# Routing of the second token group spread over chunks 9 to 15, slot positions kept as 16-bit integers

## The chip, the cores and the metric

One core of one Trainium2 chip runs the whole program. The metric is device time in microseconds of one execution. The kernel before takes 329.79 us (median of three runs, 329.2 to 330.83).

## The reference

For x of 32 x 256 tokens of 128 features (8192 tokens):

```python
xn = layernorm(x)
# s: a gated linear recurrence along each sequence of 256 tokens
hidden, gate = split(xn @ W_hg)                # 256 each
h = scan(h' = (1 - sigmoid(gate)) * h + sigmoid(gate) * (relu(hidden) + 0.5))
s = h @ W_out
# g: a shared expert plus the two best of 16 experts for each token
shared = silu(xn @ Sg) * (xn @ Su) @ Sd
p, i = top_k(softmax(xn @ Wr), 2)
routed = sum over the two of p * (silu(xn @ Wg[i]) * (xn @ Wu[i]) @ Wd[i])
out = x + s * silu(routed + shared)
```

(The recurrence is written in log space in the reference; this is what it amounts to.)

## The kernel before

**First stage: 16 chunks of 512 tokens.** PE transposes the normalised tokens, computes the router's logits (`logits`, L897) and six products of 128 x 512 for each chunk (`up`, L911: four for the recurrence, two for the shared expert), and then, one chunk later, the two down products (`rec_down`, L929, and `shared_down`, L941). ACT computes the tanh, relu and copies (`rec_in`, `shared_silu`, `copy_down`). DVE does two scans for each chunk (`rec_scan`, L551: one combining instruction at L555, one scan at L561) and the product of the shared expert (`shared_gated`, L564). The products of `up` go round four PSUM banks, so the fourth product of a chunk, `up(i, 3)`, waits for `shared_gated(i - 1)` (L917 to L925).

**Routing, in the same stage, on DVE.** The tokens are two groups: chunks 0 to 9 (40 tiles of 128 tokens) and chunks 10 to 15 (24 tiles). For each token the two best experts are found in batches of tiles (`route_top`, `route_second`, both through `first_of`, which ends with a `tensor_reduce`, L575 to L608): six and four instructions for a batch. `route_keys` turns the two experts into one of 20 lines (each line is four experts whose weights lie side by side, and any two experts share a line). `count_keys` marks the line of each token and counts along the tiles; `prefix` on PE (L950) sums over partitions; `key_bases` and `positions` turn counts into the row (slot) that each token gets in a table in DRAM. `positions` works on [128, lines, tiles] and ends with a maximum over the lines, read with a step of 24 words (L790). `shift_logits`, ACT's `exponentials` and `probabilities` give the two weights. `tile_keys` says which line each tile of 128 slots uses. For group 1 the two halves' positions are in chunks 7 and 8, for group 2 in chunk 13. What DVE does in which chunk is an order written out by hand (L832 to L874); the routing steps stand in front of the chunk's two scans. DVE, like every engine here, executes its instructions in order.

**Dispatch and slots.** POOL writes each tile's token rows to their slots, one indirect DMA for each tile (`dispatch`, L344), at most four in flight, the 40 of group 1 as soon as its positions are there (`s_pos`), then `block_weights(1)`, then the 24 of group 2, which also need `s_pos` 3. After that POOL stores results (`store_out`, L350), two indirect DMAs for each pair of slot tiles.

**Second stage: 42 pairs of slot tiles.** SP loads pair n from the table into one of RX = 10 buffers (`load_slots`, L255): pair 0 needs all dispatches of group 1, pair 10 all dispatches of group 2, and every pair n of 10 or more needs the stores of pair n - 10 to have landed:

```python
if n == PAIRS0:
    for k in range(WINDOW):
        sp.wait_ge(s_disp[k], 16 * (NT // WINDOW))
if n >= RX:
    sp.wait_ge(s_out[n % RX], 32 * (n // RX))
```

ACT normalises the rows (L457, pair n + 2 in iteration n), PE transposes them (L974) and multiplies with the line's weights (L998), ACT and DVE form the hidden values, PE transposes and multiplies down (L1010, L1023), DVE and ACT make the output rows (L816 to L825), POOL stores them.

Of the kernel before, what the change touches and what calls it, by code (L numbers as in the profile page):

```python
# [5 lines left out]
F32 = mybir.dt.float32  # L6
BF16 = mybir.dt.bfloat16
U32 = mybir.dt.uint32
I32 = mybir.dt.int32
ALU = mybir.AluOpType  # L10
ACT = mybir.ActivationFunctionType
AX = mybir.AxisListType

P = 128
# [50 lines left out]
LINES = 20  # L65
# [9 lines left out]
def recurrent_moe_block(nc, x, W_front, W_tail, W_lines, out, S, E, F):  # L75
# [14 lines left out]
        return min(2, USED - 2 * n)  # L90

    assert SLOTS % 4 == 0 and FULL_TILES * P <= len(TILES[0]) * P - LINES * (P - 1)
    BATCHES = [(0, 12), (12, 20), (20, 28), (28, 36), (36, 40), (40, 52), (52, 64)]
    HALVES = [[(0, 20), (20, 40)], [(0, 24)]]

    x_tiles = x.rearrange("(c t p) d -> c p t d", p=P, t=TT)
# [3 lines left out]
    with ExitStack() as ctx:  # L100
        def sb(name, shape, dt=F32):
            return ctx.enter_context(nc.sbuf_tensor(name, shape, dt))
# [9 lines left out]
        rev = sb("rev", [P, E])  # L112
        iota4 = sb("iota4", [P, BLOCK], U32)
        iota_k = sb("iota_k", [P, LINES], U32)
        tile_row = sb("tile_row", [P, 1])
# [47 lines left out]
        TB = max(b - a for a, b in BATCHES)  # L163
# [4 lines left out]
        r01 = sb("r01", [P, 2, NT])  # L168
        i01 = sb("i01", [P, 2, NT], U32)
        k_a, k_b, k_c, k_d, k_e = (sb(f"k_{n}", [P, TG], U32) for n in "abcde")  # L170
        key = sb("key", [P, NT], U32)
# [4 lines left out]
        oh = sb("oh", [P, LINES, TG + 1], BF16)  # L176
# [8 lines left out]
        base = sb("base", [P, LINES])  # L185
        delta = sb("delta", [P, LINES])
        fresh = sb("fresh", [P, LINES])
        moved = sb("moved", [P, LINES, 24])
        ptmp = sb("ptmp", [P, LINES, 24])
        eq = moved.rearrange("p l t -> p (l t)")[:, 0:TB * E].rearrange("p (t e) -> p t e", e=E)  # L190
        lg2 = ptmp.rearrange("p l t -> p (l t)")[:, 0:TB * E].rearrange("p (t e) -> p t e", e=E)
        pos = sb("pos", [P, NT], U32)
        le = sb("le", [P, 3, LINES])
        tk = sb("tk", [P, 3])
# [20 lines left out]
        s_step = sem("routing_step")  # L215
# [313 lines left out]
        def _(dve):  # L529
# [61 lines left out]
            def route_top(q):  # L591

                nonlocal steps
                a, b = BATCHES[q]
                n = b - a
                revs = rev[:, :].rearrange("p (t e) -> p t e", t=1).to_broadcast([P, n, E])
                dve.wait_ge(s_lgc, b // TT)
                first_of(q, lg[:, a:b], m0, 0)
                nc.vector.tensor_tensor(eq[:, 0:n], revs, per_expert(r01[:, 0, a:b], n), ALU.is_equal).then_inc(s_step, 1)
                dve.wait_ge(s_step, steps + 1)  # L600
                nc.vector.scalar_tensor_tensor(out=lg2[:, 0:n], in0=eq[:, 0:n], scalar=-BIG, in1=lg[:, a:b],
                                               op0=ALU.mult, op1=ALU.add).then_inc(s_step, 1)
                steps += 2
                dve.wait_ge(s_step, steps)

            def route_second(q):
                a, b = BATCHES[q]
                first_of(q, lg2[:, 0:b - a], m1, 1)  # L608
# [42 lines left out]
            def shift_logits(g):  # L651

                t = TILES[g]
                a, b, n = t.start, t.stop, len(t)
                nc.vector.tensor_tensor(p01[:, 1, a:b], m1[:, a:b], m0[:, a:b], ALU.subtract)
                nc.vector.tensor_tensor(lg[:, a:b], lg[:, a:b], per_expert(m0[:, a:b], n), ALU.subtract).then_inc(s_shf, 1)
# [109 lines left out]
            def positions(g, k):  # L766

                nonlocal steps
                a, b = HALVES[g][k]
                n, t0 = b - a, TILES[g].start  # L770
                dve.wait_ge(s_pref, (len(HALVES[0]) if g else 0) + k + 1)

                def per_tile(v):
                    return v[:, :].rearrange("p (l t) -> p l t", t=1).to_broadcast([P, LINES, n])

                prefix = p_lg[:, 0:LINES * n].rearrange("p (l t) -> p l t", l=LINES)
                rank, extra = ptmp[:, :, 0:n], moved[:, :, 0:n]
                nc.vector.tensor_tensor(extra, prefix, per_tile(room), ALU.subtract).then_inc(s_step, 1)
                nc.vector.tensor_tensor(rank, prefix, per_tile(base), ALU.add).then_inc(s_pread, 1)
                dve.wait_ge(s_step, steps + 1)  # L780
                nc.vector.scalar_tensor_tensor(out=extra, in0=extra, scalar=0.0, in1=per_tile(delta), op0=ALU.is_ge,
                                               op1=ALU.mult).then_inc(s_step, 1)
                dve.wait_ge(s_step, steps + 2)
                dve.wait_ge(s_pread, (len(HALVES[0]) if g else 0) + k + 1)
                nc.vector.tensor_tensor(rank, rank, extra, ALU.add).then_inc(s_step, 1)
                dve.wait_ge(s_step, steps + 3)
                nc.vector.tensor_tensor(rank, rank, oh[:, :, 1 + a:1 + b], ALU.mult).then_inc(s_step, 1)
                steps += 4
                dve.wait_ge(s_step, steps)
                nc.vector.tensor_reduce(pos[:, t0 + a:t0 + b], rank.rearrange("p l t -> p t l"), AX.X, ALU.max)\  # L790
                  .then_inc(s_pos, 1)

            def block_gated(n):
# [38 lines left out]
            for i in range(NCH):  # L832
                if 1 <= i <= 5:
                    route_top(i - 1)
                    route_second(i - 1)
                if i == 5:
                    shift_logits(0)
                if i == 6:
                    count_keys(0)
                if i == 7:  # L840
                    key_bases(0)
                    positions(0, 0)
                if i == 8:
                    positions(0, 1)
                if i == 9:
                    tile_keys(0)
                    route_top(5)
                    route_second(5)
                if i == 10:
                    route_top(6)  # L850
                    route_second(6)
                if i == 11:
                    shift_logits(1)
                    route_keys(1)
                if i == 12:
                    count_keys(1)
                if i == 13:
                    key_bases(1)
                    positions(1, 0)
                if i == 14:  # L860
                    tile_keys(1)
                for c in STATS.get(i, []):
                    ln_stats(c)
                rec_scan(i, 0)
                if i == 5:
                    route_keys(0)
                rec_scan(i, 1)
                if read(i):
                    copy_logits(read(i))
                if i == 6:  # L870
                    probabilities(0)
                shared_gated(i)
                if i == 12:
                    probabilities(1)  # L874
            for n in range(PAIRS):
                block_gated(n)
                if n >= 2:
# [234 lines left out]
```

## Time and profile before

| what | value |
|---|---|
| median of the runs | 329.79 us |
| the profiled execution's own time | 327.45 us |
| its span | 325.7 us |
| mean granted TensorE clock | 0.974 |
| busy PE, DVE, ACT, POOL | 90%, 77%, 74%, 62% of the span |
| POOL's 64 dispatches (L348) | 71.4 us busy, 1116 ns each |
| share of the chain that ended last | PE 78%, ACT 5%, issue 5%, POOL 4%, DVE 3% |

```
PE   0699999999989999996968999999999999999920
DVE  7399999999999799999451778787878787878830
ACT  1789999999975777985664777777787878787520
POOL 3997446530137776878667777665656566656670
PEclk9999999999998999998999999999999999999985
```

Each digit is one of 40 equal slices of the span (8.14 us each), the busy share in tenths, 9 for 90% and more; PEclk is TensorE's granted clock in tenths. The first stage ends at about 167 us, in slice 21. "Idle before" and names in brackets say what ended an engine's idle time. Instructions follow each other in pipelines, so the step from one start to the next is what counts, not always the printed duration.

### The profile page before, as it was taken

To read this page: it belongs to the slowest core of one execution; us is meant where nothing else is said; L and a number is where in the kernel's file an instruction comes from. 1 tells how busy PE (TensorE), PEld (TensorE's weight loads), DVE (VectorE), ACT (ScalarE), POOL (GpSimd) and SP (SyncE) were. 2 spreads that over 40 slices of the span, in tenths; PEclk is the share of its full clock that TensorE was granted. 3 is DMA by queue.
4 is the path that set the end of the run, shared out by engine and by line. 5 is a ranking of instruction groups with operands and counts; after the bars stand their busy time and mean duration, and the time that the engine had idled before them with its cause. 6 is when DMAs were issued, how large, how long until landed. Compare 5 with 4: busy or idle time off the path is not lost.

```text
span 325.7 us, 5997 instructions
## 1 busy us (share of the span) xinstructions
PE 291.7 (90%) x1523; PEld 198.5 (61%) x1523; DVE 252.0 (77%) x634; ACT 241.4 (74%) x517; POOL 201.2 (62%) x242
## 2 busy tenths in 40 slices
PE   0699999999989999996968999999999999999920
PEld 0357767766656666663645676777777777777620
DVE  7399999999999799999451778787878787878830
ACT  1789999999975777985664777777787878787520
POOL 3997446530137776878667777665656566656670
PEclk9999999999998999998999999999999999999985
DMA  8999999690006885333795435755656454541000
GB/s 233 303 372 393 440 445 399 228 432 3 0 28 204 279 256 215 124 127 147 247 405 195 168 107 194 208 176 149 180 149 181 150 181 129 168 127 51 19 0 0
DMA packets 28256, 63.62 MB, mean 195 GB/s; under 512 B 3717, under 2 KB 22672, under 8 KB 27456
## 3 DMA queue, kind: packets, MB, share of 16 engines
q1 hardware_dynamic: 21184, 45.58, 41.3%
q0 software_dynamic: 6752, 17.06, 14.2%
q10 hardware_dynamic: 288, 0.60, 0.6%
q8 instruction: 15, 0.25, 0.3%
q14 instruction: 17, 0.14, 0.1%
HBM read 29.32 MB, written 35.14 MB: 198 GB/s over the span
## 4 chain that ended last, share of the span: by engine, by line
PE 78%; ACT 5%; issue 5%; POOL 4%; DVE 3%; DMA 1%; POOLq 0%; ACTq 0%; DVEq 0%
PE p_u L998 21%; PE p_u L926 20%; PE p_s L1023 10%; PE p_s L937 8%; PE p_sh L1010 5%; PE p_lg L907 4%; PE p_sh L946 4%; PE p_xt L974 3%; POOL out L354 2%; PE p_xt L894 2%; DMA arena<-in_x 1%; POOL arena L310 1%; ACT arena L457 1%; ACT rec L427 1%; ACT rec L420 1%
## 5 line engine op out<-in xcount | busy, mean ns | idle before, releaser
L354 POOL DMA_INDIRECT out<-arena x83 | 82.1, 989 | 46.4 <-DVE arena L825 30.0
L926 PE MATMUL p_u<-xT,w_front 128*128 128x512 f32 x192 | 93.9, 622 | 3.2 <-DVE prod L569 2.5
L348 POOL DMA_INDIRECT slots<-arena,pos x64 | 71.4, 1116 | 28.7 <-issue 16.1
L998 PE MATMUL p_u<-arena 128*128 x166 | 78.3, 593 | 0.0
L926 PEld LDWEIGHTS p_u<-xT,w_front 128*128 128x128 f32 x192 | 34.9, 198 | 35.4 <-issue 33.9
L1023 PEld LDWEIGHTS p_s<-arena,rec 128*128 128x128 f32 x332 | 43.4, 191 | 21.2 <-issue 21.2
L799 DVE TENSOR_TENSOR rec<-p_u,rec 128x512 f32<-128x512 f32 (+1 forms) x42 | 28.8, 685 | 29.3 <-ACT rec L473 29.3
L480 ACT ACTIVATE rec<-p_sh 128x512 f32<-128x512 f32 (+1 forms) x42 | 24.9, 592 | 30.8 <-PE p_sh L1010 30.8
L1023 PE MATMUL p_s<-arena,rec 128*128 x332 | 44.1, 276 | 1.3 <-ACT rec L480 1.3
L998 PEld LDWEIGHTS p_u<-arena 128*128 128x128 f32 x166 | 28.3, 190 | 19.6 <-issue 19.6
L561 DVE TENSOR_TENSOR_SCAN rec<-rec 128x512 f32<-128x512 f32 x32 | 39.3, 1229 | 1.1
L937 PEld LDWEIGHTS p_s<-w_tail,rec 128*128 128x128 f32 x256 | 31.7, 195 | 8.3 <-issue 8.3
L457 ACT ACTIVATE arena<-arena 128x128 f32<-128x128 f32 x83 | 36.3, 490 | 0.0
L937 PE MATMUL p_s<-w_tail,rec 128*128 128x128 f32 x256 | 31.7, 278 | 0.0
L808 DVE TENSOR_TENSOR rec<-rec,arena 128x256 f32<-128x256 f32 x83 | 31.2, 417 | 0.1
L405 ACT ACTIVATE xn<-arena 128x128 f32<-128x128 f32 x64 | 25.9, 490 | 6.7 <-POOL arena L314 6.7
L473 ACT ACTIVATE rec<-p_u 128x512 f32<-128x512 f32 (+1 forms) x42 | 24.8, 592 | 2.1 <-PE p_u L998 2.0
L1010 PE MATMUL p_sh<-ident,rec 128*128 128x128 f32 x166 | 25.0, 273 | 0.0
L555 DVE SCALAR_TENSOR_TENSOR rec<-rec 128x512 f32<-128x512 f32 x32 | 22.0, 687 | 3.6 <-ACT rec L429 3.4
L823 DVE TENSOR_TENSOR arena<-arena 128x256 f32<-128x256 f32 (+1 forms) x42 | 17.7, 422 | 8.5 <-ACT arena L486 8.4
L424 ACT ACTIVATE rec<-p_u 128x512 f32<-128x512 f32 x32 | 19.0, 593 | 7.1 <-PE p_u L926 6.4
L307 POOL TENSOR_TENSOR var_eps<-meanvar,eps 128x4 f32<-128x4 f32 x16 | 7.1, 445 | 25.1 <-DVE meanvar L542 23.9
(130 smaller groups left out, 440.5 us busy)
## 6 DMA issues: line engine op xcount, KB each, us to landing
slots<-arena SPq DMA_DIRECT2D x4, 4116.0 KB, 27.0
arena<-slots SPq DMA_DIRECT2D x41, 392.0 KB, 3.3
arena<-in_W_lines SPq DMA_DIRECT2D x2, 2304.0 KB, 11.3
arena<-in_x SPq DMA_DIRECT2D x16, 256.0 KB, 5.3
arena<-in_W_lines SPq DMA_DIRECT2D x4, 768.0 KB, 4.5
out<-arena POOLq DMA_INDIRECT x83, 2.7
slots<-arena,pos POOLq DMA_INDIRECT x64
w_front<-in_W_front ACTq DMA_DIRECT2D x1, 392.0 KB, 3.6
```

The lines of the kernel that those rows point to most:

```text
L348: pool.indirect_dma_start(slots, index, xrow[:, t], None).then_inc(s_disp[t % WINDOW], 16)
L354: pool.indirect_dma_start(out, index, xg[:, n % RX, h, X], None, bounds_check=T - 1, oob_is_err=False)\
L405: last = nc.scalar.activation(xn[:, c % XN, t], row[:, X], ACT.Identity, bias=row[:, NBIAS:NBIAS + 1], scale=row[:, RSTD:RSTD + 1])
L457: last = nc.scalar.activation(xs[:, n % 2, h], row[:, X], ACT.Identity, bias=row[:, NBIAS:NBIAS + 1], scale=row[:, RSTD:RSTD + 1])
L561: nc.vector.tensor_tensor_scan(rec_h[:, c % 2, j], rec_a[:, j], rec_v[:, j], 0.0, ALU.mult, ALU.add)\
L799: nc.vector.tensor_tensor(hg[:, 0:m], p_u[:, b:b + m, 2 * P:4 * P], sil[:, n % 2, 0:m], ALU.mult).then_inc(s_hg, 1)
L808: last = nc.vector.tensor_tensor(hw[:, n % 2, h].rearrange("p (b f) -> p b f", b=BLOCK), hg[:, h].rearrange("p (b f) -> p b f", b=BLOCK), ...
L926: nc.tensor.matmul(p_u[:, n % 4], w_front[:, UPS[q]:UPS[q] + P], xT[:, c % XB], start=True, stop=True)\
L937: last = nc.tensor.matmul(p_s[:, t * P:(t + 1) * P], rec_h[:, c % 2, j, t * P:(t + 1) * P], w_tail[:, j * P:(j + 1) * P], start=j == 0, st ...
L998: last = nc.tensor.matmul(p_u[:, n % 2 * 2 + h], xsT[:, n % 2, h * P:(h + 1) * P], w_lines[:, bass.DynSlice(line_at[2 * n + h], 4 * P)], s ...
L1010: last = nc.tensor.transpose(p_sh[:, (2 * h + b) * P:(2 * h + b + 1) * P], hw[:, n % 2, h, b * P:(b + 1) * P], ident[:, :])
L1023: last = nc.tensor.matmul(p_s[:, h * P:(h + 1) * P], hT[:, n % 2, 2 * h + b], w_lines[:, bass.DynSlice(at + (4 + b) * P, P)], start=b == 0 ...
```

## The change

Three things are changed. The last two batches of top-two search (tiles 40 to 52 and 52 to 64) become one of 24 tiles, whose first half is done in chunk 9 and whose second in chunk 10. The other routing steps of group 2 are placed in chunks 10 to 15: `shift_logits(1)` one chunk earlier, `probabilities(1)` in front of `key_bases(1)` in chunk 13 where it stood behind the product of chunk 12, `positions(1, 0)` and `tile_keys(1)` one chunk later. And in `positions`, for both groups, the rank and the step are 16-bit integers; the masked rank is written transposed, tiles before lines, so that the last maximum reads it in one run. The scratch tiles of the search no longer share memory with those of `positions`.

```diff
-    BATCHES = [(0, 12), (12, 20), (20, 28), (28, 36), (36, 40), (40, 52), (52, 64)]
+    BATCHES = [(0, 12), (12, 20), (20, 28), (28, 36), (36, 40), (40, 64)]
...
-        moved = sb("moved", [P, LINES, 24])
-        ptmp = sb("ptmp", [P, LINES, 24])
-        eq = moved.rearrange("p l t -> p (l t)")[:, 0:TB * E].rearrange("p (t e) -> p t e", e=E)
-        lg2 = ptmp.rearrange("p l t -> p (l t)")[:, 0:TB * E].rearrange("p (t e) -> p t e", e=E)
+        eq = sb("eq", [P, TB, E])
+        lg2 = sb("lg2", [P, TB, E])
+        rank_l = sb("rank_l", [P, LINES, 24], I16)
+        step_l = sb("step_l", [P, LINES, 24], I16)
+        rank_t = sb("rank_t", [P, 24, LINES], I16)
...
-                rank, extra = ptmp[:, :, 0:n], moved[:, :, 0:n]
+                rank, extra, own = rank_l[:, :, 0:n], step_l[:, :, 0:n], rank_t[:, 0:n]
...
-                nc.vector.tensor_tensor(rank, rank, oh[:, :, 1 + a:1 + b], ALU.mult).then_inc(s_step, 1)
+                nc.vector.tensor_tensor(own.rearrange("p t l -> p l t"), rank, oh[:, :, 1 + a:1 + b], ALU.mult).then_inc(s_step, 1)
...
-                nc.vector.tensor_reduce(pos[:, t0 + a:t0 + b], rank.rearrange("p l t -> p t l"), AX.X, ALU.max)\
+                nc.vector.tensor_reduce(pos[:, t0 + a:t0 + b], own, AX.X, ALU.max)\
...
                 if i == 9:
                     tile_keys(0)
                     route_top(5)
+                if i == 10:
                     route_second(5)
-                if i == 10:
-                    route_top(6)
-                    route_second(6)
+                    shift_logits(1)
                 if i == 11:
-                    shift_logits(1)
                     route_keys(1)
                 if i == 12:
                     count_keys(1)
                 if i == 13:
+                    probabilities(1)
                     key_bases(1)
+                if i == 14:
                     positions(1, 0)
-                if i == 14:
+                if i == 15:
                     tile_keys(1)
...
                 shared_gated(i)
-                if i == 12:
-                    probabilities(1)
```

## Rows read from the trace of the kernel before

**Rows 1.** The chain of waits around chunks 13 to 15 (start us, us, what).
```profile
152.30 2.04 PE p_u L926 x2
154.34 2.31 PE p_s L937 x16
...
157.54 5.15 PE p_u L926 x12
162.70 1.78 PE p_s L937 x16
```

**Rows 2.** The timeline of PE, chunks 13 and 14 (idle time and its releaser in brackets).
```profile
145.38 4.46 PE L926 MATMUL p_u<-xT,w_front 128*128 128x512 f32 x10
152.30 2.04 PE L926 MATMUL p_u<-xT,w_front 128*128 128x512 f32 x2 [2.46 <-DVE prod L569]
```

**Rows 3.** Stretches of PE: us, busy, granted clock, DMA share, GB/s.
```profile
152.00:153.00 1.00, 0.70 (x1) 0.50 0.12 47
170.00:171.00 1.00, 0.47 (x3) 1.00 1.10 423
```

**Rows 4.** The timeline of DVE, chunks 12 and 13.
```profile
139.99 0.69 DVE L569 TENSOR_TENSOR prod<-p_u,silu_s 128x512 f32<-128x512 f32 x1
...
143.39 0.66 DVE L778 TENSOR_TENSOR moved<-p_lg,room 128x480 f32<-128x480 f32 x1
...
145.90 0.66 DVE L787 TENSOR_TENSOR ptmp<-ptmp,oh 128x480 f32<-128x480 f32 x1
146.60 1.27 DVE L790 TENSOR_REDUCE pos<-ptmp 128x24 uint32<-128x480 f32 x1
147.79 0.68 DVE L555 SCALAR_TENSOR_TENSOR rec<-rec 128x512 f32<-128x512 f32 x1
...
151.49 0.67 DVE L569 TENSOR_TENSOR prod<-p_u,silu_s 128x512 f32<-128x512 f32 x1
```

**Rows 5.** The timeline of DVE, durations by width and type.
```profile
85.50 0.81 DVE L669 TENSOR_REDUCE esum<-lg 128x40 f32<-128x640 f32 x1
...
92.04 1.09 DVE L790 TENSOR_REDUCE pos<-ptmp 128x20 uint32<-128x400 f32 x1
...
109.16 0.36 DVE L583 TENSOR_TENSOR moved<-lg,m 128x192 f32<-128x192 f32 x1
...
125.32 0.55 DVE L656 TENSOR_TENSOR lg<-lg,m 128x384 f32<-128x384 f32 x1
...
133.84 0.26 DVE L694 TENSOR_SCALAR oh<-oh 128x320 bf16<-128x320 bf16 x1
```

**Rows 6.** The chain of waits, chunks 7 and 8.
```profile
95.52 1.52 issue
...
97.70 4.13 PE p_u L926 x6
```

**Rows 7.** The timeline of DVE, end of chunk 7.
```profile
96.74 0.20 DVE L548 COPY lg<-p_lg 128x64 f32<-128x64 f32 x1
```

**Rows 8.** The timeline of POOL, first dispatch of either group and first store.
```profile
94.11 1.87 POOL L348 DMA_INDIRECT slots<-arena,pos  x1 [5.69 <-DVE pos L790]
...
155.25 1.62 POOL L348 DMA_INDIRECT slots<-arena,pos  x1 [0.28 <-POOL arena L365]
...
190.18 1.06 POOL L354 DMA_INDIRECT out<-arena  x1 [0.30 <-issue]
```

**Rows 9.** The waits of SP's queue from 186 to 215 us.
```profile
SPq L263 <- DMA out<-arena: 2.3, 1, 2.3
```

**Rows 10.** SP's load of pair 11: its issue, and its time to landing.
```profile
198.16 0.36 SPq L266 DMA_DIRECT2D arena<-slots  x1
...
DMA to landing us min/median/max: 3.2/3.2/3.2
```

**Rows 11.** The timeline of ACT, pair 11's normalisation.
```profile
203.50 0.87 ACT L457 ACTIVATE arena<-arena 128x128 f32<-128x128 f32 x2
```

**Rows 12.** The timeline of PE, pair 11's transpose.
```profile
205.50 0.38 PE L974 MATMUL p_xt<-ident,arena 128*128 128x128 f32 x2
```

More of the change, by code:

```diff
@@ L8 @@
 U32 = mybir.dt.uint32
+I16 = mybir.dt.int16
 I32 = mybir.dt.int32
```

## The prediction

> **What bounds the kernel now.** I read the chain of waits first. It is PE for 78% of the span, and in the first stage it leaves PE for long at two places only. The first is chunk 7 to 8: 1.52 us in which nothing shown holds PE's prefix product back [rows 6]; DVE's copy of the logits of chunk 14 ran at 96.74 for 0.20 us [rows 7], and the prefix waits for it (`s_lgc` 15), so DVE is what was late. The second is chunk 13 to 14: PE sat idle 2.46 us before 152.30 until `shared_gated(13)` [rows 2].
>
> Then I read DVE's timeline to see why. After `shared_gated(12)` at 139.99 DVE went on with probabilities, bases and positions of group 2, and only at 147.79 with the scans of chunk 13; `shared_gated(13)` came at 151.49 [rows 4]. So one chunk carried 147.79 - 140.68 = 7.1 us of routing. A chunk without logits takes PE 7.8 us (5.15 for six products, 1.78 and 0.89 for the down products [rows 1]) and its scans and product take DVE 151.49 + 0.67 - 147.79 = 4.4 us, so about 3.4 us of routing fit.
>
> Each gap costs twice. At the end of the second one the granted clock of PE is 0.50, that is 1.2 of 2.4 GHz [rows 3], after 2.46 us without a matmul. One product took 2.04 us where six take 5.15 (0.86 each), and the 16 down products took 2.31 where they take 1.78 [rows 1]: 1.18 + 0.53 = 1.71 us. In chunk 8 three products took 4.13 us [rows 6] instead of 2.58, which is 1.55 more.
>
> Last I read what could hold the second stage if it started earlier: POOL's dispatches and stores, SP's waits and the first pairs of slots that reuse a buffer [rows 8 to 12].
>
> **The change, part by part.** *One batch instead of two.* A batch of 12 tiles is 10 instructions of 0.36 us on 192 columns [rows 5], 0.39 from start to start; two batches 7.8 us. A batch of 24 tiles works on 384 columns, 0.55 us [rows 5], 0.59 with the same 0.03 between: 5.9 us. 1.9 us of DVE go. What they free in chunks 9 and 10 is worth nothing to the end, since PE runs there without a gap; the cover is PE's own 7.8 us a chunk.
>
> *The spread.* Routing per chunk becomes: chunk 9 six instructions of 0.59 and `tile_keys(0)`, which it has now too; chunk 10 four and `shift_logits(1)`, 3.0; chunk 11 what it has now without `shift_logits(1)`; chunk 12 what it has now; chunk 13 from 140.68 to 143.39, 2.7 [rows 4]; chunk 14 the positions, 147.79 - 143.39 = 4.4 [rows 4]; chunk 15 `tile_keys(1)`, eight instructions on 60 columns and less, under 0.36 each [rows 5]. Chunks 9 to 12 have no gap now and get less work or the same. Chunk 13: the scans start at 143.4, and have to wait for ACT's two inputs and for PE's sixth product of chunk 13. Five products start at 145.38 and end at 149.7 [rows 2], so the second of them is done at 147.1; `shared_gated(13)` can then run to 147.8, and PE wants its bank at 149.7. It is 1.9 us early instead of 2.5 late. Chunk 14: positions from 147.8 to 152.2, scans and product 4.4 more, done at 156.6. PE, not held, reaches `up(14, 3)` at 149.7, and `up(15, 3)` one chunk of 7.8 later, 157.5: 0.9 us of room. So the gap of 2.46 and the clock's 1.71 both go: PE ends the first stage 4.17 us earlier. The cover of chunk 14 is thin: positions longer by over 0.9 us would open a new gap. Chunk 15's small step has chunk 15's 3.4 us to itself.
>
> New waits: none, but `s_pos` 3, for POOL's second group, moves from 147.9 to about 152.2. Its first dispatch is at 155.25, behind group 1's last [rows 8], so 3 us of cover remain. `s_toff` 2 moves by one chunk; its reader is pair 10, over 40 us later. Nothing moves past SP's or POOL's queue, and no DMA is added.
>
> *The 16-bit positions.* Six instructions for a half; for 400 columns L778, L779, L781 (PSUM or fp32 operands) I leave as they are. L785 has only 16-bit operands: 0.57 now; the nearest 16-bit row, a one-source instruction, takes 0.26 for 320 columns [rows 5]; I take 0.4, between 0.26 and 0.57. The mask multiplication now writes with a step of 20 elements of 2 bytes; no row shows such a write. The nearest is the maximum that reads with a step of 24 words, 1.09 us for 400 columns [rows 5]; in one run the reduction of 640 takes 0.81 [rows 5], which scales to about 0.57 for 400. So bounds for the multiplication are 0.57 (the step costs a write nothing; below that, 0.4, if it also runs at a 16-bit rate) and 1.09 (as the read), and, if a write suffers twice what the read does, 1.6. I take 1.09. The maximum becomes 0.57. Sum for 400 columns: 0.57 + 0.57 + 1.09 = 2.23 now, 0.4 + 1.09 + 0.57 = 2.06 then: 0.2 us gained, between 0.9 gained and 0.5 lost.
>
> The Trainium skill ("Vector Engine (DVE) Microarchitecture Reference", Measured stream behaviour on trn2) lists a destination that steps 24 words every element at 2.5 ns a column, like two sources that do so, against 1.05 in one run. By it the transposed write gives back what the maximum gains, which speaks against this part; a write without a penalty would make the gain 0.7. The read's 1.09 us agrees with it, and no run here shows the write.
>
> What the 0.2 us is worth: positions(0, 0) stands in front of the gap of 1.52 in chunk 7, so PE's gap becomes 1.3, and POOL's first dispatch moves from 94.11 [rows 8] to 93.9. Whether the clock still falls after 1.3 us is open: from 170 to 171 us PE was idle for over half the time and still granted 1.00, that is 2.4 GHz [rows 3]. I take that it falls as before.
>
> *Where the 4.4 us arrive.* I take the first pairs' rows to be there as much earlier as PE asks. The tight place is the reuse of buffers. POOL dispatches from 94.11 and starts the first store only at 190.18, released by nothing but its own queue [rows 8]: it does not follow PE. SP waited 2.3 us for that store before pair 10's load [rows 9], and issued pair 11's at 198.16, landed 3.2 us later, 201.4 [rows 10]. ACT wants it at 203.50 [rows 11], takes 0.87, and PE wants the result at 205.50 [rows 12]: 2.1 + 1.1 = 3.3 us of room. POOL's chain gains only the 0.2 us. PE's 4.4 us therefore are cut to 3.3 + 0.2 = 3.5; about 0.9 us reappears as an idle PE at pair 10 or 11. From there POOL has less work for each pair than PE (6 to 7 tenths busy against 9 in the slices shown with the profile), so it catches up and the end follows PE.
>
> Sum: 327.45 - 3.5 = 323.95 us for an execution like the profiled one. The median of the runs lies 2.34 us above the profiled execution; I carry the difference over: **326.3 us**.
>
> **The rivals.** *The whole shift arrives, 0.17.* The stores' landing times may close up, or a POOL that is disturbed less by DVE may be earlier. With the clock of chunk 8 back as well, 4.17 + 0.2 + 1.55 = 5.9: 323.9 us. Against it: POOL would have to be over 2 us earlier.
>
> *A second clock loss, 0.20.* If the new gap at pair 10 is longer than 0.9 us and the clock falls there, about 1.7 us goes: 3.5 - 1.7 = 1.8, 328.0 us. For it: both long gaps of the first stage lost the clock; against it: the stretch at 170 us did not [rows 3].
>
> *The ring of buffers binds already, 0.15.* The timed runs are 2.3 us longer than the profiled one. If what is longer is POOL's chain, the room of 3.3 us is only 1 in them, and the gain is 1.2 or less: 328.6 to 329.6 us.
>
> *Slower, 0.08.* POOL's chain itself grows. Its first dispatch took 1.87 us and the first of group 2 1.62 [rows 8], where the mean of the 64 is 1.12. Eight more such lengthenings by 0.6 us would put the first store 4.8 us later; from 3.5 us on, pairs 10 and 11 come later than before. At 4.8: 331.1 us. That DVE's work is moved against POOL's speaks for it; that it is less work in sum speaks against. The Trainium skill ("SBUF — State Buffer") has DVE instructions with two SBUF inputs exclude a GpSimd instruction that reads SBUF. By it the new batch would hold POOL as long as its columns last, which are as many as before.
>
> *The transposed write is worse than any row, 0.05.* At over 1.0 us more per positions, chunk 14 opens a gap again and chunk 8's grows: about 329.5 us.
>
> **How the numbers follow.** The forecast of 3.5, between 2.8 and 4.2 with the bounds of the positions and the landings, has 0.35. About 0.5% (1.65 us) is what a measurement here can tell from no change. Faster by more: the forecast, the whole shift, and most of the second clock loss, 0.35 + 0.17 + 0.18 = 0.70. Within 0.5%: 0.15 + 0.02 + 0.05 = 0.22. Slower: 0.08. The range goes from 324.2, in the middle of the first rival, to 329.4, leaving out about 0.08 on either side.
>
> **What would show it.** Right: no idle PE between 142 and 162 us, and none of its clock at 0.50 there; chunk 14's product not late; the last product of chunk 15 about 4.4 us earlier; the first store within 0.5 us of 190; idle PE of about 1 us near 200, waiting for ACT's L457 and that for SP's load. In positions: L785 near 0.4, the multiplication near 1.1, the maximum near 0.6. Wrong: a store chain that moves by more than 1 us either way, a gap in chunk 14, or PE's second stage unchanged after an earlier start with no wait for a load.

## The result, and the profile after

The changed kernel takes 330.01 us (median of 20 executions, 328.18 to 334.1) against 329.31 us for the kernel before beside it (20 executions, 324.52 to 331.17); the ratio is 1.0095, 95% interval 1.0067 to 1.0123. It is slower by 1% or less, where I forecast 3.5 us faster. The ratio leaves out executions over 1.5% above the fastest of their kernel, 9 of the 20 before and 1 of the 20 after, since the kernel before scatters by 2%; so I also give plain means over all executions, with a 95% interval from resampling them: 330.4 us (329.7 to 331.2) against 328.5 (327.7 to 329.4), a loss of 1.9 us (0.8 to 3.1). The two agree in sign; the ratio would make it 3.1 us. The profiled execution took 329.06 us, its span is 327.3 against 325.7.

From the page of the changed kernel, PE's busy tenths and its granted clock in 40 slices, the chain that ended last by engine, then two groups (line engine op, busy us and mean ns, idle before and its releaser):

```profile
PE   0699999999979999999967996999999999999920
...
PEclk9999999999998999999999998899999999999975
...
PE 64%; POOL 15%; issue 8%; DMA 6%; ACT 3%; DVE 1%; POOLq 1%; ACTq 0%; SPq 0%
...
L350 POOL DMA_INDIRECT slots<-arena,pos x64 | 75.7, 1183 | 28.8 <-issue 14.6
...
L459 ACT ACTIVATE arena<-arena 128x128 f32<-128x128 f32 x83 | 36.3, 489 | 4.4 <-DMA arena<-slots 4.4
```

Slice 19, where PE had its long gap (6 tenths busy, clock 8 before), is full now. Slice 25 is new with 6 tenths, and so are the clock's 8s in slices 25 and 26, 196 to 213 us; the clock's 8 in slice 13 is chunk 7's, as before. POOL holds 15% of the chain that ended last, where it held 4%, and PE 64% instead of 78%. The 64 dispatches take 75.7 us instead of 71.4, and ACT waits 4.4 us for loads of slots, where it waited for none.

PE's timeline, the idle pieces (in brackets) that changed:

```profile
97.63 0.49 PE L960 MATMUL p_lg<-oh,tri 128*128 128x400 bf16 x1 [1.78 <-issue]
...
158.25 1.10 PE L926 MATMUL p_u<-xT,w_front 128*128 128x512 f32 x2 [0.33 <-DVE prod L571]
...
165.30 0.44 PE L974 MATMUL p_xt<-ident,arena 128*128 128x128 f32 x2 [1.56 <-ACT arena L459]
...
202.08 0.44 PE L974 MATMUL p_xt<-ident,arena 128*128 128x128 f32 x2 [2.63 <-ACT arena L459]
```

The gap of 2.46 us [rows 2] is 0.33 now and keeps its clock; the gap of chunk 7 grew from 1.52 [rows 6] to 1.78. The first transpose of a slot tile (L974) comes at 165.30; in the trace before it came at 168.66. So 3.36 us of the forecast's 4.4 did arrive in the first stage. At 202.08 PE then sits idle 2.63 us for ACT's L459, which is L457 of [rows 11].

DVE's timeline of the changed kernel, the last three steps of `positions(0, 0)`, to be held against the 0.57 and 1.09 us of before [rows 5]:

```profile
90.79 0.37 DVE L787 TENSOR_TENSOR rank_l<-rank_l,step_l 128x400 int16<-128x400 int16 x1
91.19 1.92 DVE L789 TENSOR_TENSOR rank_t<-rank_l,oh 128x400 int16<-128x400 int16 x1
93.14 0.57 DVE L792 TENSOR_REDUCE pos<-rank_t 128x20 uint32<-128x400 int16 x1
```

And chunks 12 to 14, the scan of chunk 12, the product of chunk 13, the masked write of group 2, the product of chunk 14:

```profile
139.06 1.22 DVE L563 TENSOR_TENSOR_SCAN rec<-rec 128x512 f32<-128x512 f32 x1
...
147.96 0.69 DVE L571 TENSOR_TENSOR prod<-p_u,silu_s 128x512 f32<-128x512 f32 x1 [0.49 <-PE p_u L926]
...
150.82 2.29 DVE L789 TENSOR_TENSOR rank_t<-rank_l,oh 128x480 int16<-128x480 int16 x1
...
157.44 0.66 DVE L571 TENSOR_TENSOR prod<-p_u,silu_s 128x512 f32<-128x512 f32 x1
```

POOL's timeline: first dispatch of group 1, two long ones, first dispatch of group 2, first store [rows 8 has three of them before]:

```profile
94.70 1.87 POOL L350 DMA_INDIRECT slots<-arena,pos  x1 [6.30 <-ACT arena L444]
...
139.21 1.84 POOL L350 DMA_INDIRECT slots<-arena,pos  x1 [0.30 <-issue]
...
151.48 1.97 POOL L350 DMA_INDIRECT slots<-arena,pos  x1 [0.30 <-issue]
...
159.71 1.31 POOL L350 DMA_INDIRECT slots<-arena,pos  x1 [0.39 <-POOL arena L367]
...
194.18 1.00 POOL L356 DMA_INDIRECT out<-arena  x1 [0.30 <-issue]
```

The store that frees the first buffer starts at 194.18 instead of 190.18. ACT's waits from 190 to 215 us, and a stretch with PE, PEld, DVE, ACT and POOL busy, then granted clock, DMA share and GB/s:

```profile
ACT arena L459 <- DMA arena<-slots: 4.4, 2, 3.8
```

```profile
203.00:204.00 1.00, 1.00 (x2) 0.43 (x2) 1.00 (x4) 0.67 (x2) 0.70 (x2) 0.50 1.00 365
```

PE's clock is 0.50, the 1.2 GHz level, after that idle piece. Summed over the stretches in which it is lowered, each such fall takes away 1.7 us of clock in these two traces, whatever the gap: before it fell after the gaps at 97 and 152 us, now at 97 and 202.

So the sum for the two profiled executions: -3.36 at the start of the second stage; then PE's transpose for pair 10 comes at 202.08 where it came at 202.24 (same line, the piece before [rows 12]), so 3.20 us are given back in front of it, 2.63 of them in one piece; then 1.7 us of clock. That is +1.5 of the +1.6 us of span.

### The profile page after: what moved, and what is told of

Read it like the earlier page. It is cut to its first block, busy times and chain, and to the rows that moved or that the text cites. A ratio compares the mean times of both kernels' runs of the same rounds, so it can differ in the third digit from the quotient of the medians.

```text
span 327.3 us, 5986 instructions
## 1 busy us (share of the span) xinstructions
PE 292.2 (89%) x1523; PEld 198.4 (61%) x1523; DVE 251.7 (77%) x624; ACT 241.7 (74%) x517; POOL 205.5 (63%) x242
## 4 chain that ended last, share of the span: by engine, by line
PE 64%; POOL 15%; issue 8%; DMA 6%; ACT 3%; DVE 1%; POOLq 1%; ACTq 0%; SPq 0%
PE p_u L926 18%; PE p_u L998 17%; POOL slots L350 10%; PE p_s L1023 9%; PE p_s L937 6%; PE p_sh L1010 4%; PE p_lg L907 4%; DMA slots<-arena,pos 3%; PE p_sh L946 3%; POOL out L356 2%; PE p_xt L974 2%; PE p_xt L894 2%; DMA arena<-in_x 1%; DMA arena<-slots 1%; POOL arena L312 1%
## 5 line engine op out<-in xcount | busy, mean ns | idle before, releaser
L350 POOL DMA_INDIRECT slots<-arena,pos x64 | 75.7, 1183 | 28.8 <-issue 14.6
L926 PE MATMUL p_u<-xT,w_front 128*128 128x512 f32 x192 | 92.3, 614 | 1.0 <-ACT xT L415 0.7
L998 PE MATMUL p_u<-arena 128*128 x166 | 79.6, 602 | 0.0
L459 ACT ACTIVATE arena<-arena 128x128 f32<-128x128 f32 x83 | 36.3, 489 | 4.4 <-DMA arena<-slots 4.4
L557 DVE SCALAR_TENSOR_TENSOR rec<-rec 128x512 f32<-128x512 f32 x32 | 21.7, 678 | 2.0 <-ACT rec L431 1.8
```

Of the source, the lines that this page charges most:

```text
L350: pool.indirect_dma_start(slots, index, xrow[:, t], None).then_inc(s_disp[t % WINDOW], 16)
L459: last = nc.scalar.activation(xs[:, n % 2, h], row[:, X], ACT.Identity, bias=row[:, NBIAS:NBIAS + 1], scale=row[:, RSTD:RSTD + 1])
L926: nc.tensor.matmul(p_u[:, n % 4], w_front[:, UPS[q]:UPS[q] + P], xT[:, c % XB], start=True, stop=True)\
L998: last = nc.tensor.matmul(p_u[:, n % 2 * 2 + h], xsT[:, n % 2, h * P:(h + 1) * P], w_lines[:, bass.DynSlice(line_at[2 * n + h], 4 * P)], s ...
```

## The experiments

Two theories were set against each other. **A**: POOL's chain sets the end. It grew, and pairs 10 and 11 wait for its stores. **B**: the longer masked write costs its time on DVE alone.

Behind A stands a reading that one can make with both traces. I laid the 40 dispatches of group 1 (L350, L348 before), each at its start plus 0.19 us, over DVE's timeline. 16 of them are over 0.96 us by 0.1 or more before, by 8.0 us in sum; 23 are after, by 12.9 us. Every one stands beside a DVE instruction with two inputs in SBUF (scan, L557, `tensor_tensor` of two SBUF tiles) that had begun before it, and ends 0.75 to 0.84 us after that instruction does (0.34 after the masked write, 1.0 for the very first). None stands beside a reduction or an instruction that reads PSUM. The scan of 139.06 and the dispatch of 139.21 above show it: 139.06 + 1.22 + 0.77 = 141.05 = 139.21 + 1.84. This rests on lining up records, but in 39 of 39 cases, and in 191 of 191 with the traces of e1 to e4 and f1 to f4. The moment decides: where such an instruction began later than 0.03 us before the dispatch, or after it, the dispatch took 0.96 us all the same, as at 113.43 in the trace of before, beside a scan that began at 113.46.

### e1: the spread alone

```diff
-        rank_l = sb("rank_l", [P, LINES, 24], I16)
-        step_l = sb("step_l", [P, LINES, 24], I16)
-        rank_t = sb("rank_t", [P, 24, LINES], I16)
+        moved = sb("moved", [P, LINES, 24])
+        ptmp = sb("ptmp", [P, LINES, 24])
```

(positions as before; batches and chunks as in the change)

> The spread and the single batch alone; positions stay fp32 and untransposed, as in the kernel before. Theory A (POOL's chain sets the end: each dispatch that begins beside a DVE instruction with two SBUF inputs is lengthened until that instruction is done, and pairs 10 and 11 wait for POOL): the first dispatch is back at 94.1 us, the 1.6 us that dispatches lost beside the transposed write are gone, so the first store is at 190 to 193 us against 194.2 in the changed kernel and 190.2 before; the first stage ends over 4 us earlier than before, and PE still sits idle 1 to 3 us near pair 10. Ratio to before 0.993 to 1.002. Theory B (the transposed 16-bit write is the whole loss, through DVE, and POOL's chain does not matter): the full 4.2 us arrive, ratio 0.986 to 0.989.

Measured: mean 327.9 us (327.1 to 328.8, 12 executions) against 328.6 (327.8 to 329.3, 35 executions of before, the same for e1 to e4); ratio 1.0039 (1.0005 to 1.0074); mean and ratio point to different sides here, so I call e1 level with before. POOL's timeline, first dispatches and first store:

```profile
94.10 1.87 POOL L349 DMA_INDIRECT slots<-arena,pos  x1 [5.70 <-DVE pos L791]
...
157.52 1.00 POOL L349 DMA_INDIRECT slots<-arena,pos  x1 [0.28 <-POOL arena L366]
...
192.82 1.11 POOL L355 DMA_INDIRECT out<-arena  x1 [0.30 <-issue]
```

The first store is at 192.8, as A has it. The gap of chunk 13 is gone, and PE has no idle piece at pair 10. That part of A's forecast (1 to 3 us idle) missed, because PE itself came late to pair 10 in this execution (ACT did wait 0.85 us for its load). Its windows (us, busy, granted clock, DMA share, GB/s) show why: the clock fell among the short pauses at the stage's end, for 3.4 us of clock.

```profile
164.00:168.00 4.00, 1.91 (x6) 0.70 1.04 400
168.00:172.00 4.00, 4.00 (x12) 0.50 1.06 409
```

In the traces of before and after the same pauses cost nothing [rows 3]; in those of e3, e4, f2 and f4 they cost 1.7 us of clock. So B's full 4.2 us did not arrive either; B's ratio of 0.989 or less lies outside both measures. But a first store 2.6 us later, with the positions as before, means that the order alone can lengthen POOL's chain: the masked write is not its only cause.

### e2: the 16-bit positions alone

```diff
-    BATCHES = [(0, 12), (12, 20), (20, 28), (28, 36), (36, 40), (40, 64)]
+    BATCHES = [(0, 12), (12, 20), (20, 28), (28, 36), (36, 40), (40, 52), (52, 64)]
```

(routing steps in the chunks of before)

> The 16-bit transposed positions alone, in the order and batches of before. Both theories: each positions call is 0.6 to 0.7 us longer (multiplication 1.9 and 2.3 us), the gap of chunk 7 grows from 1.5 to about 2.1 us, that of chunk 13 from 2.5 to about 3.1, the end comes 1.2 to 2 us later: ratio 1.003 to 1.008. Theory A adds that the first store moves later by 0.6 us plus what dispatches lose beside the longer multiplication (0 to 2 us), and that this alone costs nothing, since PE is 1.3 us later too and 3.3 us of room were there.

Measured: mean 329.9 us (329.0 to 330.8), ratio 1.008 (1.0039 to 1.0121). PE's two gaps, then POOL's first store:

```profile
97.79 0.49 PE L962 MATMUL p_lg<-oh,tri 128*128 128x400 bf16 x1 [1.78 <-issue]
...
153.42 1.10 PE L928 MATMUL p_u<-xT,w_front 128*128 128x512 f32 x2 [3.23 <-DVE prod L571]
```

```profile
193.68 1.10 POOL L356 DMA_INDIRECT out<-arena  x1 [0.31 <-issue]
```

Both grew, the first to 1.78 us (expected 2.1), the second to 3.23 (expected 3.1). The second one, longer than any of the trace of before, kept its clock: the product behind it took 1.10 where it took 2.04 [rows 1]. The first store is 3.5 us later than before, more than the 0.6 to 2.6 that A had; PE, at pair 9 only 0.4 us earlier than before, still had no idle piece at pair 10, and ACT waited 0.87 us for its load: the room was all but used. The 16-bit transposed positions are a loss by themselves, 1.4 us of the mean (0.2 to 2.5).

### e3: the change without the transposed write

```diff
-                nc.vector.tensor_tensor(own.rearrange("p t l -> p l t"), rank, oh[:, :, 1 + a:1 + b], ALU.mult).then_inc(s_step, 1)
+                nc.vector.tensor_tensor(rank, rank, oh[:, :, 1 + a:1 + b], ALU.mult).then_inc(s_step, 1)
...
-                nc.vector.tensor_reduce(pos[:, t0 + a:t0 + b], own, AX.X, ALU.max)\
+                nc.vector.tensor_reduce(pos[:, t0 + a:t0 + b], rank.rearrange("p l t -> p t l"), AX.X, ALU.max)\
```

> The whole change, but the masked rank is written in place, lines before tiles, and the maximum reads it with a step of 24 elements of 2 bytes. The multiplication should take about 0.37 us for 400 columns (all operands 16-bit, in runs) instead of 1.92, the maximum 1.1 (as fp32 reads with a step now) to 1.9 us (as the transposed write). So a positions call is 0.3 us shorter to 0.4 longer than before, and the multiplication no longer stands beside dispatches for long. Theory A: first store at 190 to 193 us, ratio 0.990 to 1.002, and like the fp32 spread within 0.3%. Theory B: ratio 0.985 to 0.989.

Measured: mean 326.3 us (325.4 to 327.2), 2.2 us under before; ratio 0.9982 (0.9941 to 1.0023). DVE's timeline, the same three steps:

```profile
93.01 0.37 DVE L786 TENSOR_TENSOR rank_l<-rank_l,step_l 128x400 int16<-128x400 int16 x1
93.41 0.38 DVE L788 TENSOR_TENSOR rank_l<-rank_l,oh 128x400 int16<-128x400 int16 x1
93.83 0.86 DVE L791 TENSOR_REDUCE pos<-rank_l 128x20 uint32<-128x400 int16 x1
```

0.37 + 0.38 + 0.86 = 1.61 us, where fp32 took 2.23 and the change 2.86. Reading with a step is far cheaper than writing with one: 0.86 against 1.92 us for the same 400 elements. PE's timeline:

```profile
98.60 0.35 PE L959 MATMUL p_lg<-oh,tri 128*128 128x400 bf16 x1 [0.89 <-issue]
...
200.56 0.44 PE L973 MATMUL p_xt<-ident,arena 128*128 128x128 f32 x2 [0.65 <-ACT arena L458]
```

The gap of chunk 7 shrank to 0.89 us and the clock did not fall there; 0.65 us of idle remain at pair 10, although the clock fell among the pauses at 167 us and made PE later. The first store is at 192.64, as A has it, in an execution that lost 2.2 us between chunks 0 and 1. B's ratio of 0.985 to 0.989 is outside; so is "like the fp32 spread within 0.3%", since e1's mean is 0.5% longer. The maximum, expected at 1.1 to 1.9 us, took 0.86.

### e4: the kernel before, POOL 2 us later

```diff
+            pool.wait_ge(s_xt, NCH)
+            for k in range(2):
+                nc.gpsimd.memset(xn[:, :, :, :], 0.0).then_inc(s_idle, 1)
+                pool.wait_ge(s_idle, k + 1)
             block_weights(1)
```

> The kernel before with two memsets of 1024 columns on POOL (about 0.9 us each) between the two groups of dispatches, so the first store is 2 us later. Theory A with the room of 3.3 us that I read from the trace of before: no idle PE at pairs 10 and 11, ratio 0.999 to 1.002. If POOL's chain binds already in the kernel before: ratio 1.004 to 1.007. Theory B: ratio 1.000.

Measured: mean 329.2 us (328.3 to 330.1), 0.6 above before (-0.5 to 1.8); ratio 1.0086 (1.0043 to 1.0128), which lies above A's range and says little here, for the reason given with the result. POOL's timeline, then PE's, then ACT's at pair 10:

```profile
96.77 1.87 POOL L349 DMA_INDIRECT slots<-arena,pos  x1 [5.69 <-DVE pos L795]
...
157.43 1.98 POOL L383 MEMSET xn<- 128x1024 f32 x2
...
160.93 1.01 POOL L349 DMA_INDIRECT slots<-arena,pos  x1 [0.39 <-POOL arena L366]
...
196.53 1.11 POOL L355 DMA_INDIRECT out<-arena  x1 [0.30 <-issue]
```

```profile
99.70 0.49 PE L965 MATMUL p_lg<-oh,tri 128*128 128x400 bf16 x1 [1.52 <-issue]
...
154.86 1.10 PE L931 MATMUL p_u<-xT,w_front 128*128 128x512 f32 x2 [2.48 <-DVE prod L574]
```

```profile
203.86 0.88 ACT L462 ACTIVATE arena<-arena 128x128 f32<-128x128 f32 x2 [1.02 <-DMA arena<-slots]
```

This execution lost 2.7 us between chunks 0 and 1 (PE's prefix at 99.70 against 97.04; the profiled executions of e3, f2, f3 and f4 lost 2.2 to 3.0 there). Without it the first store is 196.53 - 190.18 - 2.7 = 3.7 us later than before, and PE, on time otherwise (two falls of the clock, as before), had no idle piece at pairs 10 or 11. But ACT waited 1.02 us for pair 10's load and took it the moment it landed, and PE came to pair 10 only 0.05 us late. So the room of the kernel before was just used up; my 3.3 was about right. Of the 3.7 us, 1.2 are not the memsets': group 1's 40 dispatches took 60.7 us from first to last here and 59.5 in the trace of before, with the same instructions up to there. The means do not tell 0.6 from nothing.

### e5 to e8: inconclusive

e5 is e4 with five memsets, e6 the change with 11 buffers, e7 the change with e4's two memsets, e8 is e3 with 11 buffers (diffs below, with f2 to f4).

> The kernel before with five such memsets on POOL between the two groups: first store about 5 us later in its own right. With two of them (first store 3.7 us later than before, measured from the first dispatch's delay) no idle PE was seen, so the room is at least about 3.7 us. Theory A: PE now sits idle 1 to 3 us near pair 10, waiting for ACT's L457 and it for the load, and may lose its clock there (1.7 us): mean 2 to 4 us above the mean of before. If POOL's chain does not matter (theory B): mean as before.

> The changed kernel with 11 buffers for pairs instead of 10 (the scratch of search and positions shares memory to make room): pair 10 waits only for the dispatches and pair 11 for the first store, about 2.3 to 2.6 us earlier than now. Theory A: the idle 2.63 us of PE near pair 10 falls under 0.6, and the clock loss behind it goes too in most executions; mean 2 to 4 us under the changed kernel's, that is 0.5 to 2 us under before. Theory B (the loss is DVE's longer positions alone): no change against the changed kernel, mean 1.5 to 2 us above before.

> The changed kernel with the two extra memsets on POOL, as e4 has them on the kernel before, where they cost 0.6 us of the mean. Theory A: here POOL's chain has no room left, so the full 1.9 us come on top: idle PE near pair 10 about 4.5 us, mean 1.5 to 2.5 us above the changed kernel, 3.5 to 4.5 above before. Theory B: no more than in e4.

> e3 (spread, 16-bit positions written in place) with 11 buffers. e3 had 0.65 and 0.24 us of idle PE near pairs 10 and 13 and a mean 2.2 us under before. Theory A: these go, mean 2.5 to 4 us under before; the best version so far. Theory B: as e3.

On this chip before had a mean of 346.0 us (29 executions, 343.7 to 348.5); e5 349.5 (346.7 to 352.6), e6 349.1 (344.6 to 353.9), e7 351.6 (346.6 to 357.9), e8 340.8 (339.0 to 343.2); ratios 1.0076 (1.0012 to 1.0139), 1.0038 (0.9973 to 1.0103), 1.01 (1.0017 to 1.0184), 0.9928 (0.9866 to 0.9989). ACT stood still between 175 and 205 us for reasons that the trace puts down to nothing on the core, as in e8:

```profile
195.77 0.60 ACT L474 ACTIVATE rec<-p_u 128x512 f32<-128x512 f32 x1 [7.00 <-remote]
```

With PE idle there for 8 to 16 us in one piece anyway, POOL's chain cannot be seen at work. By the means e5 is where A has it (3.5 us above before), e7 and e8 go A's way and beyond its ranges (5.6 above, 5.1 under), e6 does not (3.1 above before); I rest nothing on the four. e6 to e8 were run again on another chip, beside the changed kernel.

### f1: the changed kernel again

> The changed kernel once more, as the yardstick for the three beside it: group 1's 40 dispatches take 61 to 64 us from first to last (63.6 in its first trace, 59.5 to 61.3 in the kernel before and the variants without the transposed write), idle PE near pair 10 of 0.5 to 2.6 us, mean 1 to 2.5 us above before. If the growth of POOL's chain was chance alone, this trace shows under 60.

Measured: mean 329.7 us (328.9 to 330.5) against 328.5 (327.8 to 329.2, 23 executions of before, the same for f1 to f4); ratio 1.0042 (1.0004 to 1.0079). POOL's and PE's timelines (PE at pairs 9 and 10):

```profile
94.63 1.87 POOL L350 DMA_INDIRECT slots<-arena,pos  x1 [6.30 <-ACT arena L444]
...
159.63 1.31 POOL L350 DMA_INDIRECT slots<-arena,pos  x1 [0.39 <-POOL arena L367]
...
194.31 1.17 POOL L356 DMA_INDIRECT out<-arena  x1 [0.30 <-issue]
```

```profile
195.58 0.38 PE L974 MATMUL p_xt<-ident,arena 128*128 128x128 f32 x2
202.34 0.44 PE L974 MATMUL p_xt<-ident,arena 128*128 128x128 f32 x2 [3.32 <-ACT arena L459]
```

Group 1's dispatches again take 63.6 us, with 12.8 us of lengthening, and PE is idle 3.32 us at pair 10 (expected 0.5 to 2.6). The growth was no chance of one execution.

### f2: the changed kernel with 11 buffers

```diff
-RX = 10
+RX = 11
...
-        xsT = carve(2 * 2 * P).rearrange("p (n w) -> p n w", n=2)
+        xsT = sb("xsT", [P, 2, 2 * P])
...
+        work = [sb(f"work{k}", [P, LINES * 24]) for k in range(2)]
+        eq, lg2 = (w[:, 0:TB * E].rearrange("p (t e) -> p t e", e=E) for w in work)
+        halves = [w[:, k * LINES * 12:(k + 1) * LINES * 12].bitcast(I16) for w in work for k in range(2)]
...
```

> e6 again: on the chip that ran e5 to e8 ACT stood still for 5 to 16 us between 180 and 205 us in every kernel, for nothing that the trace names, which hides what POOL's chain does. The changed kernel with 11 buffers. Theory A: idle PE near pair 10 under 0.6 us; mean 1 to 3 us under the changed kernel's beside it. Theory B (longer positions alone): no difference.

Measured: mean 328.5 us (327.5 to 329.4), 1.2 under f1 (0.0 to 2.5) and level with before; ratio 0.9987 (0.9944 to 1.003). ACT's waits from 190 to 215 us, then POOL's first store and PE at pair 9:

```profile
ACT arena L459 <- DMA arena<-slots: 0.4, 1, 0.4
```

```profile
197.85 1.00 POOL L356 DMA_INDIRECT out<-arena  x1 [0.30 <-issue]
...
201.42 0.38 PE L974 MATMUL p_xt<-ident,arena 128*128 128x128 f32 x2
```

PE has no idle piece there at all, as A has it, but this trace cannot carry that. PE came to pair 9 at 201.42, 5.8 us later than in f1, and only 2.8 of them are this execution's late start (prefix at 100.34 against 97.56); the rest is the clock's, which was lowered twice as long at 99 us and fell once more among the pauses at 171. The first store is 0.8 us later than f1's on the same count. With f1's timetable for PE, pair 10's load, which now waits for the dispatches alone and was issued at 200.10, would still have come about 2 us late: an estimate from the landing at 203.19 here, less 2.8, and from f1's 195.58. So the eleventh buffer moves pair 10's load by 1 to 2 us only, and whether it takes away idle time of this kernel is not shown. B forecast no difference; the 1.2 us of the means barely speak against it. What decides is f3.

### f3: the changed kernel, POOL 2 us later

(e4's lines on the changed kernel)

> e7 again: the changed kernel with 1.9 us more on POOL between the groups. Theory A: idle PE near pair 10 grows to 3 to 4.6 us; mean 1.5 to 2.5 us above the changed kernel's beside it (in the kernel before the same cost 0.6). Theory B: no more than 0.6.

Measured: mean 333.5 us (331.9 to 335.1, 6 executions), 3.8 above f1 (2.0 to 5.5); ratio 1.0133 (1.0065 to 1.0202). POOL's first store, and PE at pairs 9 and 10:

```profile
199.61 1.10 POOL L357 DMA_INDIRECT out<-arena  x1 [0.30 <-issue]
...
198.66 0.38 PE L979 MATMUL p_xt<-ident,arena 128*128 128x128 f32 x2
207.61 0.69 PE L979 MATMUL p_xt<-ident,arena 128*128 128x128 f32 x2 [5.52 <-ACT arena L464]
```

The first store is 5.30 us later than in f1 and PE at pair 9 is 3.08 later, so POOL fell behind PE by 2.2 us more; and the idle piece is 5.52 us, 2.2 more than in f1. Behind it 3.4 us of clock are lost instead of 1.7. Idle time and mean are both above A's ranges (3 to 4.6, 1.5 to 2.5) and far from B's (0.6 at most). What cost the kernel before 0.6 us or nothing costs the changed kernel all of itself and a clock loss on top. That is POOL's chain as the bound.

### f4: e3 with 11 buffers

(f2's lines for the buffers; positions as in e3)

> e8 again: spread, 16-bit positions written in place, 11 buffers. Theory A: no idle PE near pairs 10 to 13, mean 2.5 to 4 us under before. Theory B: as e3, 2.2 us under before.

Measured: median 324.78 us, mean 324.2 (322.8 to 325.4, 6 executions), 4.3 under before and 5.5 under the changed kernel; ratio 0.9873 (0.9811 to 0.9936). PE and its clock from the page:

```profile
PE   0699999999998999999968999999999999999920
...
PEclk9999999999999999999989999999999999999995
```

No clock is lost at the gaps of chunks 7 and 13, and none near pair 10; 1.7 us are, in slice 21, among the pauses at 167 us. This version beats both kernels, by more than A's 2.5 to 4 us. It differs from f2 only in how the masked rank is written and read, so with 11 buffers the transposed write costs 4.3 us (2.8 to 5.9) of the mean. That is not POOL's chain alone: the gap of chunk 7 is 0.90 us here and kept its clock, in f2 it is 1.78 and lost it. How much of its lead over e3 (on another chip) is the eleventh buffer's was not measured alone.

## Why the prediction was wrong

**What bounds the kernel: right.** The gap of chunk 13 went from 2.46 to 0.33 us and its clock loss with it. The first stage ends 3.36 us earlier; with the 0.59 us by which PE's prefix product came later at chunk 7 (97.63 against 97.04), and the 0.33, that is the 4.17 of the forecast to 0.1 us.

**The one batch and the spread: right, with less room than forecast.** `shared_gated(13)` was done at 148.65 (forecast 147.8), having waited 0.49 us for a PE that was itself 0.6 late; `shared_gated(14)` at 158.10 (forecast 156.6), and 0.33 us of gap came of it. The 1.5 us are that delay and the masked write in about equal parts.

**The 16-bit positions: mis-sized, the first step that failed.** "I take 1.09" for the masked multiplication: it took 1.92 us for 400 columns and 2.29 for 480, above even the outer bound of 1.6. L787 at 0.37 and the maximum at 0.57 were right. So positions is 0.6 us longer, not 0.2 shorter, and POOL starts at 94.70 instead of 93.9. The row of a strided read was the wrong neighbour for a strided write, as e3 shows: 0.86 against 1.92. The Trainium skill ("Vector Engine (DVE) Microarchitecture Reference", Measured stream behaviour on trn2) puts two sources that step 24 words and a destination that does on one level, 2.5 ns a column. The one-source read here is near it (1.09 us, 2.7 ns a column); for 2-byte elements with a step of 40 bytes the write measured here is at 4.8 ns a column, nearly twice that.

**Where the 4.4 us arrive: the place was right, the length of POOL's chain was not.** "POOL's chain gains only the 0.2 us" is the step that decided. It grew by 4.0 us: 0.6 from the later start and 4.9 in lengthened dispatches of group 1 (12.9 against 8.0), less 1.5 elsewhere, of which 0.9 is less lengthening in group 2 (1.2 against 2.1). Of the 4.9, 1.6 us stand beside the masked write (two dispatches). The room of 3.3 us, which e4 bears out, was thus used up by POOL while PE came 3.4 earlier. From the forecast of -3.5 to the +1.6 us of the profiled executions it is 5.1 us: 1.0 that the first stage fell short (3.36 for 4.4), 2.3 more given back at pair 10 (3.20 for 0.9) and 1.7 of clock. I had the growth of POOL's chain as the slower rival, at 4.8 us and 331.1, and gave it 0.08, against it that DVE's work is less in sum; lining the lengthened dispatches up with DVE's instructions would have shown what they follow, in the trace that I had. The Trainium skill ("SBUF — State Buffer", Who interferes with whom), which I cited beside that rival, has the exclusion between two-input DVE instructions and GpSimd's reads; the trace agrees: the lengthened dispatches end 0.75 to 0.84 us after the instruction.

**The second clock loss: right in place and size.** 1.7 us at 202 to 206 us, a rival at 0.20. It came together with POOL's growth; my cases took them one at a time.

**The 2.34 us carried over: probably a late start.** The executions of before lie at 324.5 to 326.2, at 327.2 to 327.8 and at 329.2 to 331.3 us. The profiled one (327.45) is of the second group; e4's, with PE on the timetable of before, took 330.30 and had a late start of 2.7 us. By the sizes it is this that separates the second group from the third, and not a longer chain on POOL, as the rival of the ring of buffers has it; no execution of the kernel before itself was profiled in the third.

**What stays open.** Of the other 3.3 us of lengthening, 2.3 stand beside scans and L557 (8.9 us against 6.6 before). Group 1's dispatches took 59.5 us before and 60.7 in e4, which has the same instructions there, 61.3 in e1, 61.1 in e2, 60.7 in e3 and f4, and 63.6, 63.6, 63.4 and 61.8 in the change, f1, f2 and f3, whose DVE instructions are the same. So the trace of before is the shortest of all, and of the 4.1 us between it and the change's, one or two can be chance: a scan that begins just before a dispatch costs it up to 0.9 us, one just behind its start nothing. The change's order tends to meet more of them; why it meets more scans than e1's, which has the same scans, no run separates. No run has the changed kernel with POOL's chain made shorter and nothing else changed. Nor was it tried why the clock falls after some gaps and not after others.

## What to carry to other kernels

When an engine is freed and the work behind it also depends on a queue that the change doesn't speed up, the gain is the queue's room; work that out, and then ask what the change does to the queue itself, down to which instructions of the other engines lengthen its own. When a layout is turned to make a read run straight, price the strided write from a strided write; here leaving the write in place and letting the maximum read with a step was 1.25 us better in each call. One more buffer where two engines' timetables meet costs little memory; the two best times here are e3's and, with 11 buffers, f4's, but what the buffer alone is worth was not measured.

## What was not expected of the hardware

- An indirect DMA issued on POOL takes 0.96 us; one that begins while a DVE instruction with two SBUF inputs is running ends 0.75 to 0.84 us after that instruction does, so it takes up to 1.84 us beside a scan in the traces of before and after; beside the masked write it ends 0.34 us after it and takes up to 1.97, and the very first ends 1.0 us after its scan (191 of 191 cases in ten traces). Where the instruction began less than 0.03 us before the dispatch, or after it, it cost nothing (76 cases). Reductions and instructions reading PSUM did not do it.
- A 16-bit two-input instruction that writes with a step of 40 bytes took 1.92 us for 400 columns; in runs it takes 0.38.
- PE's clock fell to 1.2 GHz after a gap of 1.52 us at 97 us and not after one of 3.23 us at 153 (e2); a fall took 1.7 us of clock, three times 3.4 (e1, f2, f3). That is part of why the kernel before scatters over 324.5 to 331.2 us: its shortest executions (324.6 to 326.2) have a mean granted clock of 0.982 to 0.985, those at 327.2 to 327.8 one of 0.974 to 0.976.
- On one of the chips every kernel was 17 to 21 us slower than on the others, with ACT standing still around 175 to 205 us for no reason in the trace.
